# A gated delta-rule block on one core: another order for the joins and key scaling of the first batch and the block turns of the last, a split input load, more idle products

## What is computed

```python
x = x + 0.5 * ffn(_layernorm(x))          # F1
x = x + attn(_layernorm(x))               # N, P, S, M
x = x + 0.5 * ffn(_layernorm(x))          # F2
# ffn:  h = silu(x W1 s1) * (x W2 s2); h = gelu(h H1 s); h = gelu(h H2 s); h W3 s
# attn: n = layernorm(x); q, k = l2norm(silu(n Wq)), l2norm(silu(n Wk)); v = silu(n Wv)
#       beta, alpha = sigmoid(n Wb), sigmoid(n Wa)      # 8 heads of 128
def step(S, inp):
    kS = einsum('bhk,bhkv->bhv', k_t, S)
    bk = (b_t[..., None] * k_t)[..., :, None]
    S = a_t[..., None, None] * (S - bk * kS[..., None, :]) + bk * v_t[..., None, :]
    o = einsum('bhk,bhkv->bhv', q_t, S)
#       x = x + o Wo; x = x + gelu(layernorm(x) W1 + b1) W2 + b2
```

## Time and profile before

| | |
|---|---|
| median of 3 runs | 1386.29 us (1383.34 to 1386.8) |
| profiled execution | 1386.23 us |
| its span | 1384.4 us |
| TensorE busy | 1351.9 us, 98% |
| VectorE busy | 858.5 us, 62% |
| ACT busy | 663.1 us, 48% |
| POOL busy | 566.1 us, 41% |
| chain that ended last | PE 71%, issue 9%, DVE 7%, POOL 7%, DMA 2%, ACT 2% |

### The profile page before, as it was taken

How to read it: one execution, slowest core, us unless ns; L and a number is a source line. 1 busy time by engine, 2 the same in 40 slices (tenths; PEclk the granted TensorE clock), 3 DMA queues, 4 the chain that set the end, 5 groups by cost and what they waited for, 6 DMA issues and landing times.

```text
span 1384.4 us, 25270 instructions
## 1 busy us (share of the span) xinstructions
PE 1351.9 (98%) x9792; PEld 929.6 (67%) x9792; DVE 858.5 (62%) x2503; ACT 663.1 (48%) x1130; POOL 566.1 (41%) x644
## 2 busy tenths in 40 slices
PE   8999999999999999999999999999999999999998
PEld 4456676658856587566875568655786658855887
DVE  4477976466774577744766558656586446775542
ACT  2476646236642456425662356622666236642233
POOL 0038343822447144560437515283144823466000
PEclk9999999999999999999999999999999999999999
DMA  6030255432564144630447315463254432640000
GB/s 187 27 97 1 82 132 115 89 81 70 130 130 94 41 100 125 133 90 30 122 99 141 89 30 125 113 108 89 61 134 101 88 74 83 141 106 31 9 1 8
DMA packets 346471, 121.47 MB, mean 88 GB/s; under 512 B 312624, under 2 KB 327728, under 8 KB 346352
## 3 DMA queue, kind: packets, MB, share of 16 engines
q1 hardware_dynamic: 346352, 119.86, 37.1%
HBM read 77.88 MB, written 41.94 MB: 87 GB/s over the span
## 4 chain that ended last, share of the span: by engine, by line
PE 71%; issue 9%; DVE 7%; POOL 7%; DMA 2%; ACT 2%; SPq 1%; POOLq 0%; DVEq 0%; ACTq 0%
PE bank L1466 23%; PE bank L1582 9%; PE bank L1495 4%; PE bank L1677 4%; PE bank L1668 4%; PE bank L1641 3%; PE bank L1607 3%; PE bank L1474 3%; PE bank L1658 3%; POOL blkT L613 2%; PE bank L1632 2%; POOL blkP L610 2%; PE bank L1649 2%; PE bank L1624 2%; PE bank L1890 1%
## 5 line engine op out<-in xcount | busy, mean ns | idle before, releaser
L1466 PE MATMUL bank<-big,h 128*128 128x512 f32 (+1 forms) x1056 | 444.2, 569 | 0.0
L1466 PEld LDWEIGHTS bank<-big,h 128*128 128x128 f32 x1056 | 194.8, 190 | 191.8 <-issue 185.8
L567 POOL TENSOR_TENSOR rnorm<-ssq,mhalf 128x16 f32<-128x16 f32 (+1 forms) x35 | 84.1, 2404 | 426.4 <-DVE ssq L877 426.4
L1582 PE MATMUL bank<-wqkv,nT 128*128 128x512 f32 x336 | 160.0, 597 | 1.1 <-ACT V L1285 1.1
L613 POOL TENSOR_TENSOR blkT<-blkT,blkP 128x31 f32<-128x31 f32 (+15 forms) x248 | 135.3, 545 | 19.4
L610 POOL TENSOR_TENSOR blkP<-blkA,blkT 128x31 f32<-128x31 f32 (+15 forms) x248 | 129.3, 522 | 29.5 <-DMA blkA<-blocks_out 10.7
L1495 PE MATMUL bank<-xT,w 128*128 128x512 f32 (+1 forms) x272 | 118.6, 579 | 8.7 <-DVE big L753 5.9
L1195 ACT ACTIVATE big<-bank,cols 128x512 f32<-128x512 f32 (+1 forms) x68 | 43.9, 662 | 133.9 <-PE bank L1466 95.8
L1203 ACT ACTIVATE big<-bank,cols 128x512 f32<-128x512 f32 (+1 forms) x68 | 44.1, 662 | 126.1 <-PE bank L1466 126.1
L1002 DVE TENSOR_TENSOR MT<-bank,MT 128x512 f32<-128x512 f32 x56 | 38.5, 691 | 100.4 <-PE bank L1624 100.4
L594 POOL TENSOR_TENSOR QET<-QET,sgf 128x1024 f32<-128x1024 f32 x24 | 56.5, 2354 | 98.3 <-DMA sgf<-e_rows 91.1
(11 more groups left out here) (239 smaller groups left out, 2433.4 us busy)
## 6 DMA issues: line engine op xcount, KB each, us to landing
rows_or_g<-g_rows SPq DMA_DIRECT2D x28, 512.0 KB, 5.0
q_rows<-mid SPq DMA_DIRECT2D x28, 512.0 KB, 4.7
QET<-q_rows SPq DMA_DIRECT2D x112, 128.0 KB, 4.2
k_rows<-R SPq DMA_DIRECT2D x27, 512.0 KB, 2.7
KT<-k_rows SPq DMA_DIRECT2D x108, 128.0 KB, 3.8
sgf<-e_rows SPq DMA_DIRECT2D x24, 512.0 KB, 4.5
blocks_out<-R SPq DMA_DIRECT2D x128, 32.0 KB, 1.7
blkA<-blocks_out SPq DMA_DIRECT2D x8, 512.0 KB, 3.8
```

What stands on the lines that cost most here:

```text
L567: pool.tensor_tensor(rnorm[:, heads_of], ssq[:, heads_of], mhalf[:, :].to_broadcast([128, heads_of.stop - heads_of.start]), ALU.pow).then_ ...
L1466: last = pe.matmul(bank[bk + i][:, t], w[:, k, 128 * o:128 * o + 128], src[:, k, t], start=(k == 0), stop=(k == KB - 1))
L1582: pe.matmul(bank[proj_bank(b, n)][:, :], nT[:, 128 * c:128 * c + 128], wqkv[:, i // 2, 512 * (i % 2):512 * (i % 2) + 512], start=True, sto ...
```

## The change

The first input load stays on SP, and the other two are issued by ACT, behind its wait for POOL's masks. `squares` is split into its statistics and its sums; in batch 0's joins the statistics of batch 1's first keys stand ahead of the last copy, and the sums behind it. In the first `SP_first`, the scaling and turning of these keys stand first, and the rows of n0 move behind the states. On TensorE and ACT the last projection of `AHEAD` moves behind the last join. In the last batch both `turn_T1` stand ahead of the first join's copies, and the last two `turn_R` ahead of the second join's copies. Idle products: 27 instead of 20 in the last overlapped step, and 20 instead of 16 at the start.

```diff
-            load_xin(0)
+            sp.dma_start(xin[:, FIRST, :], rows_of(d["x"], 0)[:, FIRST, :]).then_inc(ld_x, 16)
...
             def squares(b, g):
+                squares_stats(b, g), squares_sums(b, g)
+            def squares_stats(b, g):
...
                 last.then_inc(p_bst, 1)
+            def squares_sums(b, g):
+                lo, hi = H if g == NC else 0, H if g == 0 else 2 * H
                 k = (b - 1) * NG + g
...
             def joins_alone():
...
-                turn_R(0, 2), joined(0, 2), cumulated(1), joined(0, 3)
-                squares(1, 0), N_rows(1, n0, 0, n_n0)
+                turn_R(0, 2), joined(0, 2), cumulated(1), squares_stats(1, 0), joined(0, 3), squares_sums(1, 0)
...
             def SP_first(s, p):
+                if p == 1:
+                    unit_k(p, 0)
                 if p is not None:
                     unit_blocks(p)
                 new_state(s, 0, 0)
...
                 new_state(s, 0, 1)
-                if p is not None:
+                if p == 1:
+                    N_rows(1, n0, 0, n_n0)
+                elif p is not None:
                     unit_k(p, 0)
                 attended(s, 0)
...
-            turn_T(B - 1), turn_R(B - 1, 1), turn_R(B - 1, 3), joined(B - 1, 0), turn_T1(1), turn_T1(3)
-            joined(B - 1, 1), turn_R(B - 1, 2), turn_R(B - 1, 0), joined(B - 1, 2), joined(B - 1, 3)
+            turn_T(B - 1), turn_R(B - 1, 1), turn_R(B - 1, 3), turn_T1(1), turn_T1(3), joined(B - 1, 0)
+            turn_R(B - 1, 2), turn_R(B - 1, 0)
+            for k in range(1, JOINS):
+                joined(B - 1, k)
...
-                for c, i in AHEAD[8:]:
-                    silu(1, c, i)
-                joined(0, 3)
+                silu(1, *AHEAD[8]), joined(0, 3), silu(1, *AHEAD[9])
...
             act.wait_ge(c_pool, 1)
+            first_rows = d["x"][0:1, :, :].rearrange("o (c p) n -> p (o c) n", p=128)
+            for p, r, k in ORDER[1:]:
+                act.dma_start(xin[p, k, :], first_rows[r, k, :]).then_inc(ld_x, 16)
             act.activation(warm[:, :], ones[:, :], ACT.Silu).then_inc(act_warm, 1)
...
-                    idle_products(bank[3], 20)
+                    idle_products(bank[3], 27)
...
-                for c, i in AHEAD[8:]:
-                    proj(1, c, i)
-                lone_join(3)
+                proj(1, *AHEAD[8]), lone_join(3), proj(1, *AHEAD[9])
...
-            idle_products(bank[7], 16)
+            idle_products(bank[7], 20)
```

## The result

The changed kernel takes 1394.17 us (median of 6 runs, 1392.59 to 1397.55) against 1386.81 us (median of 6, 1383.34 to 1390.1): a ratio of 1.0057, 95% interval 1.0045 to 1.0069. By the medians it is 7.4 us slower, by the ratio 7.9 us, where I forecast about 3.9 us less. The profiled execution took 1396.53 us.

A forecast was written before the change was run, and what follows sets the result against it. TensorE, busy 98% of the span, was taken to bound the kernel, so only its waits and clock falls count. Sum: 1386.2 + 1.3 (input) - 2.3 (keys) - 2.8 (last batch) = 1382.4 us; range 1380.3 to 1386.0.

The forecast's parts named there:

- Part 1: Start: two input loads on ACT are issued later and land later, +1.3 us, bounds +0.7 to +3.2.
- Rival D: Start: input held up behind the weights, 5.2 us late, layer 1 at the lower clock (1.9): 1388.2 us; chance 0.10.
- Cost nothing: Start: the 4 added idle products take 0.9 us but end before the transposes can start, so no cost.
- Part 2: First batch: earlier key scaling removes the 2.42 us wait before the key products, solve 0.15 us later: gain 2.3 us.
- Parts 3 and 4: Last batch: more idle products prevent a clock fall, reordered turns remove the 2.07 us wait: gain 2.8 us together.
- B: The clock falls in a new gap, in the last batch or at the start: 1383.7 to 1384.3, both 1385.6; chance 0.27.
- C: Start: the input is not later, because fewer loads share a queue: 1381.1 us; chance 0.12.
- E: First batch: keys gain little, through a wait for the states or a late load back: 1384.7 us; chance 0.11.
- A: Whole kernel: the forecast itself, 1382.4 us, own range 1381.3 to 1383.6; chance 0.40.
- expected signs: First statistics at 5.6 us, keys 3.4 us earlier without wait, layer 1 clock 1.00, slot 13 wait 2.4, last batch 57.8.
- three conditions for being wrong: Input delay over 3 us, granted clock falling twice in new places, or a wait for the states at 167 us.

The follow-up runs named there:

- b_input_act: The kernel before, with only two of the three input loads moved to ACT behind its wait for the masks: 1393.42 us, ratio 1.005.
- a_weights_behind: The changed kernel, with SP holding its first weight load until all three input loads are there: 1385.69 us, ratio 0.9999 to the kernel before.
- a_idle48: The changed kernel with 48 idle products at the start instead of 20: 1394.88 us, ratio 1.0065 to the kernel before.
- b_idle20: The kernel before, only with 20 idle products at the start instead of 16: 1387.9 us, ratio 1.0013.
- c_idle16: a_act_no_wait with 16 idle products at the start instead of 20: 1384.23 us, ratio 0.9982 to the kernel before.
- b_keys: The kernel before, with only the first batch's part (statistics split, key scaling first, n0 rows later, last projection and SiLU moved): 1385.01 us, ratio 0.9988.
- a_act_no_wait: The changed kernel, with ACT issuing its two input loads ahead of its wait for the masks: 1385.55 us, ratio 0.9994 to the kernel before.
- best: The changed kernel with its whole start as before (three input loads on SP, 16 idle products): 1384.37 us, ratio 0.9987 to the kernel before.
- best_nomove: best with the last projection and its SiLU ahead of the last join again: 1383.46 us, ratio 0.9985 to the kernel before.
- b_last: The kernel before, with only the last batch's part (27 idle products and the order of turns): 1386.14 us, ratio 1.0002.
- b_turns: The kernel before, with only the last batch's new order of block turns: 1385.01 us, ratio 0.9994.

## Why the prediction was wrong, point by point

**Part 1, the loads (predicted +1.3, bound +3.2; measured +6.9 by b_input_act alone, interval 4.9 to 9.1, and 8.9 at layer 2 in its trace).** This is the step that failed: "I take +1.3 us, near the lower end", with the landing at most doubled. The issue times were right; the landing was 4.2 to 6.7 us, up to three times the 2.3 us of the earlier trace rows. I priced the landing by loads that stood ahead of the weights in the order of one queue, and moved them to where they are served side by side with the weights. The row with the right size was at hand, 6.6 us for a load among the weights, and I set it aside since it stood "in SP's own queue behind 2 MB". a_weights_behind shows that the queue isn't the point, the other packets are. Rival D named this mechanism, gave 5.2 us of delay (measured 5.46) and had 0.10; that was too little. Its time, 1388.2, was 6 us short all the same, mainly since it kept the last batch's gain, had the lower clock too cheap and left the idle products at nothing.
On the page DMA: Bandwidth & Descriptors of the Trainium skill, the section Issuing engines are not separate DMA queues says that transfers of different issuers run on the same DMA engines and interleave. The trace agrees, with q1 at 76% and q10 at 11% of the same 16 engines in 4 to 6 us. I had drawn from this page that the upper bound was the likelier, and still took a value near the lower; and the bound itself, twice the landing, was too low.

**The clock at the start.** D counted 1.9 us for layer 1 at the lower clock; it was 3.4 (11.84 against 8.44 us). After standing idle for 6.25 us TensorE ran the transposes and layer 1's first 5.9 us at 1.2 GHz. In b_input_act, after 7.95 us, it was the same; in a_idle48, with 0.30 us of idle time, the clock stayed at 1.00.

**"Cost nothing" for the 4 idle products at the start.** This was right for the start itself and wrong for the kernel: +1.8 us (b_idle20), 1.7 us the other way (c_idle16). b_idle20's trace loses 2.4 us between 330 and 1230 us, 0.9 of them by the late store of the keys and 0.8 at 471 us; the rest comes in smaller steps that I didn't follow.

**Part 2, the keys (predicted -2.3; measured -1.7, interval -0.4 to -2.8).** The mechanism was right: the wait is gone, the states are not late, and the store's way is as computed. Two terms are off in size. The solve is late by 0.55 us instead of 0.15: from the short products ahead of the first join (line 1964) it is 18.00 to 18.07 us, in the profiles without a fall there, against 17.46 to 17.51. In the changed kernel ACT's SiLU, put behind its share of the copy, ends at 170.16 us, and the solve starts 0.25 us later. It starts as closely behind this SiLU in b_keys, a_act_no_wait and best, though the bracket in best names VectorE's copy; and best_nomove, where only the projection and this SiLU are moved back, is at 17.46. And the old wait of 2.42 us was on the large side: b_last has 2.07, b_turns 1.82, b_idle20 1.60, b_input_act 1.32.

**Parts 3 and 4, the last batch (predicted -2.8; measured +0.3 and -0.8, both intervals across zero).** In the profiles the stretch did become 2.6 us shorter, 60.59 to 57.95 us, as predicted (57.8). But two falls of the clock were in the 60.59, and they are not there in every execution: b_input_act and b_idle20 have the same last batch as the kernel before, with the same waits (1.25 to 1.27 and 2.09 us) and no fall, and take 58.00 and 58.04 us. The rest of the 60.59 is the price of the falls. From the transposes to layer 2 it is 10.00 us in the kernel before and 8.98 in b_idle20, and from slot 18 to the solve 4.69 against 3.15. So the falls cost 1.0 and 1.5 us, where I had 1.9 and 1.5. The order itself is worth 0.1 to 0.7 us. I had read one execution's falls as a property of the place.

Over the 14 profiles a fall of some 3.4 us was seen at 58 to 67 us in seven, at 150 to 181 us in six, at 1175 us in one, in the last batch in three and at 1338 to 1342 us in four; c_idle16 and b_idle20 have none before the end. The fall behind the 2.09 us wait came in two of the four profiles with the old order and in none of the ten with the new. The new order may thus make it rarer, but b_last (-1.0 to +1.7 us) and b_turns (-2.1 to +0.3 us) show no gain from it.

The falls are also a large part of the spread of the times. For the 93 executions of the kernel before in the three sessions the mean granted clock is on record. The median time is 1383.3 us where it is 1.000 (5 executions), 1386.1 at 0.998 (37) and 1388.4 at 0.996 (13), some 1.1 us for each 0.001.

**The sum.** The parts measured alone give, by their ratios, +6.9 (loads) + 1.8 (idle products at the start) - 1.7 (keys) + 0.3 (last batch) = +7.3 us, against 7.9 by the ratio of the whole change. Each part is known to 1 or 2 us only, so that they meet this closely is in part luck. The first term alone, +6.9 in place of +1.3, makes my sum 1388.0, outside the range. A further 3.1 us are the last batch's gain that wasn't there, 1.8 the idle products and 0.6 the keys; that gives 1393.5 us, where 1394.17 was measured.

**The rivals.** B's falls in new gaps happen, but elsewhere and in some runs only. C (input not later) is excluded. E let the keys gain next to nothing (2.3 us less than A); 0.6 us less were measured, and no wait for the states appeared. The expected signs held in part: turned keys early (5.6 us behind the solve, before 9.2), no wait at the key products, a wait ahead of slot 13 (1.20 for 2.4 us) and none over 0.6 later, 57.95 for 57.8 us. The one that decided, VectorE's first statistics at 5.6 us or with D at 9.6, came out at 9.81. Of my three conditions for being wrong, two came true: the input is more than 3 us later, and the clock fell in new places (at 12.6, 67 and 159 us).

## What to carry to other kernels

A small load that the first work waits for should be ahead of the bulk loads in time, not merely on another queue, since its packets share the DMA engines with whatever is moving. Put it first, and if it can't be first, hold the bulk back for it. A fall of the clock that one profile shows at a place is no fixed price of that place: look at a second execution, or at a kernel that shares the stretch, before booking it as a gain. Idle instructions are code too, and 4 more of them cost this kernel 1.8 us far from where they stand, so a change of their number is to be measured for itself.

## What was unexpected of the hardware

- 64 KB loads issued at 2.3 to 3.1 us beside the weights landed after 4.2 to 8.0 us in three kernels; with the weights held back, after 2.4 to 2.5 us; issued at 0.8 to 1.5 us, after 2.6 to 3.6 us in two kernels.
- After TensorE stood idle for 6.25 us the granted clock was 0.50 for 10.2 us (12.6 to 22.8), though work had resumed at 14.95; after 7.95 us (b_input_act) also for 10.2 us.
- The short falls to 0.50 last 3.4 us each and come at the same few places in kernels whose work there is the same, but in some executions and not in others. In the last batch of the kernel before they cost 1.0 and 1.5 us.
- A 512 KB store (at 331.7 us in the kernel before) takes 2.7 to 2.9 or 4.2 to 5.0 us by the number of idle products some 330 us earlier, and one VectorE operation of 128x4 elements at 462 us takes 0.7 to 1.3 or 1.5 to 2.1 us by the same number.
